# Two of six second layers in three reduced-precision products, and a new order around them, in the last stage of a fused graph and expert network

## The chip, the cores and the metric

The kernel runs on one core of a Trainium2 chip. The metric is the device time of one execution in microseconds, here the median of several runs. The inputs are 8192 tokens of 128 channels (128 graphs of 64 nodes) and an adjacency matrix per graph.

## The reference

Two rounds, each a graph layer and an expert layer, each on a layer norm of the stream `x` and added to it. The last expert layer is the one that matters here:

```
xn = layernorm(x)
rh = relu(xn @ router_w1 + router_b1)
p  = softmax(rh @ router_w2 + router_b2)          # 6 experts
top_w, top_i = top_k(p, 2);  g = softmax(top_w)
h1 = relu(xn @ expert_w1[e] + expert_b1[e])       # 128 -> 128, all e
h2 = relu(h1 @ expert_w2[e] + expert_b2[e])       # 128 -> 128
o  = h2 @ expert_w3[e] + expert_b3[e]             # 128 -> 128
x  = x + sum over the two chosen e of g * o[e]
```

The graph layer before it multiplies the normed stream by the weight and the degree-normed adjacency of each graph.

## The kernel before, in words

The program has three parts: the first round's graph layer, attention and router (to about 260 us), the first expert layer in 71 blocks of 256 slots (to about 535 us), and the last stage, which does the second round's graph layer and its dense expert layer over 16 groups of 512 tokens. The change lies in the last stage, and a little in the preparation of its weights on GpSimd during the blocks.

In the last stage every engine runs its own loop `body(g, p)` over steps. A step holds work of several groups: `g[0]` is the newest, `g[1]` the one before it, and so on. Each operation is a small function that first waits on semaphores and then issues its instructions, and the order in `body` is the order in the engine's queue. VectorE's and GpSimd's steps are numbered two ahead: what is `g[2]` there is `g[0]` in TensorE's step at the same time. The names, for one group:

- graph layer: `aT` (TensorE, adjacency), `tT` (ScalarE copies it out of PSUM), `gnn` (TensorE), `x3` (VectorE adds it to the stream), `st1`, `mv1`, `var1` (VectorE, statistics), `rstd1` (GpSimd, writes `rs_d`), `f3` (VectorE, the normed stream), `f3T` (TensorE, transposes), `hi` (ScalarE) and `lo` (VectorE), which split it into a high and a low half in fp32r; `pick`, `add0`, `add1`, `st0`, `mv0`, `var0` (VectorE), `rstd0` (`rs_c`), `xb` and eight gathers `gt` (GpSimd), `scale` and `xn` (VectorE) prepare the next group's graph layer.
- router: `rh` (TensorE), `rhr` (ScalarE), `logits` (TensorE), a chain of small operations on VectorE with `etop` and `ep` on ScalarE between them, down to `gate`, `ghi`, `glo`; then `gateT` (TensorE) and `gTc` (ScalarE).
- experts, n = 0 to 5: `a(n)` is the first layer, always three fp32r products (high by high, high by low, low by high; line 2205), `ra(n)` (ScalarE, line 1455) its bias and relu into `h1[n % 3]`; `b(n)` is the second layer, one fp32 product, which the trace shows as two records (line 2229), `rb(n)` (ScalarE, line 1462) its bias and relu into `h2[n % 3]`; `m(n)` (VectorE, line 1804) multiplies by the broadcast gate; `c(n)` (TensorE, line 2237) is the third layer, fp32, added up over n in one bank; `eb` adds the last biases, `oTc`, `oT`, `ob` bring the result back and add it to the stream.

An operation reuses a buffer or a PSUM bank as soon as its last reader has signalled. `h1` has three buffers, so `ra(n)` waits for `b(n - 3)` of the same group, or `b(n + 3)` of the group before. The first layers of experts 4, 2 and 1 are computed one step ahead (`a(4, g[0])`, `a(2, g[0])`, `a(1, g[0])` at the end of TensorE's step), but `ra(4)` runs only in the next step, behind `hi`.

The order in TensorE's step: aT, a(0), c(1), c(2), gnn, gateT, c(3), b(0), c(4), a(3), c(5), a(5), eb, b(1), oT, f3T, b(2), b(3), rh, b(4), a(4), logits, a(2), b(5), c(0), a(1).

Of the kernel before, what the change touches and what calls it, by code (L numbers as in the profile page):

```python
# [20 lines left out]
P = 128  # L21
NB, NN, C = 128, 64, 128
TOK = NB * NN
TG = 4
# [72 lines left out]
def build(nc, x, adj_t, gnn0_w, gnn0_b, ln1, ln2, wqkv, wo, router0, w13, w2, gnn1_w, gnn1_b,  # L97
# [19 lines left out]
    with ExitStack() as whole:  # L117
# [906 lines left out]
        with ExitStack() as ctx:  # L1024
# [41 lines left out]
            tile_aT, tile_tT, tile_gnn = sem("tile_aT"), sem("tile_tT"), sem("tile_gnn")  # L1066
            AHEAD = LOOPED + 5
            DEG_BLOCK, degrees = 8, sem("degrees")
            PREPARED = 8 + TG - 1
            st_a, mv_a, var_a, rs_a = sb("st_c", [P, TG, 6]), sb("mv_c", [P, TG, 2]), sb("var_c", [P, TG]), sb("rs_c", [P, TG])  # L1070
            st_b, mv_b, var_b, rs_b = sb("st_d", [P, TG, 6]), sb("mv_d", [P, TG, 2]), sb("var_d", [P, TG]), sb("rs_d", [P, TG])
            rhT = sb("rhT", [P, GT])
# [2 lines left out]
            z, zr, pk, dp, ep, e1 = sb("z_c", [P, TG]), sb("zr", [P, TG]), sb("pk", [P, TG, 2]), sb("dp", [P, TG]), sb("ep", [P, TG]), sb("e1", [P, TG])  # L1075
            rk, ohr, gate = sb("rk", [P, TG, 2]), sb("ohr_c", [P, TG, 2, 8]), sb("gate", [P, TG, 32])
            h1 = [w[:, 1, 0:2, :].rearrange("p c r -> p (c r)") for w in (act1, prod)] + [sb("h1_2", [P, GT])[:, :]]
            h2 = [f[:, :, :].rearrange("p t c -> p (t c)") for f in flat] + [act1[:, 0, 0:2, :].rearrange("p c r -> p (c r)")]
            h2g = [xs[:, 0:2, :, :].rearrange("p u t c -> p (u t c)"), ys[:, :, :, :].rearrange("p u t c -> p (u t c)"),
                   prod[:, 0, 0:2, :].rearrange("p c r -> p (c r)")]  # L1080
            oT = sb("oT", [P, GT])
            gateT = [sb(f"gateT{i}", [P, P]) for i in range(2)]
            gateS = [sb(f"gateS{i}", [P, GT], f32r) for i in range(2)]
            spare, spare2 = sb("spare_c", [P, 1]), sb("spare_d", [P, 8])
# [20 lines left out]

            per = {n[0].rstrip("012345"): Steps(sem("per_" + n[0]), " ".join(n)) for n in (
                ("a4", "a2", "a1", "a0", "a3", "a5"),
                ("ra2", "ra0", "ra1", "ra3", "ra4", "ra5"),
                ("b0", "b1", "b2", "b3", "b4", "b5"),
                ("rb0", "rb1", "rb2", "rb4", "rb3", "rb5"),  # L1110
                ("m0", "m1", "m2", "m3", "m4", "m5"),
                ("c0", "c1", "c2", "c3", "c4", "c5"))}

# [2 lines left out]
            def reused(engine, by, n, g):  # L1116

                if n >= 3:
                    engine.wait_ge(per[by].sem, per[by].at(f"{by}{n - 3}", g))
                elif has(g - 1):  # L1120
                    engine.wait_ge(per[by].sem, per[by].at(f"{by}{n + 3}", g - 1))
# [23 lines left out]
            def later(g, n):  # L1145
                return None if isinstance(g, int) and g < n else g
# [32 lines left out]
            with nc.Block() as block:  # L1179
# [103 lines left out]
                def _(pool):  # L1283
# [16 lines left out]
                    def weights():  # L1300
# [21 lines left out]
                        pool.wait_ge(ld_w, 16 * NW)  # L1322
                        for high, w in ((ew1_hi, ew1), (rw1_hi, rw1), (eb3_hi, eb3)):
                            G.tensor_copy(high[:, :], w[:, :]).then_inc(prepared, 1)
                        pool.wait_ge(prepared, 4)
                        for low, w, high in ((ew1_lo, ew1, ew1_hi), (rw1_lo, rw1, rw1_hi), (eb3_s, eb3, eb3_hi)):
                            G.tensor_tensor(low[:, :], w[:, :], high[:, :].bitcast(f32), ALU.subtract).then_inc(prepared, 1)
                        pool.wait_ge(prepared, 7)
                        G.tensor_copy(eb3_s[0:16, :], eb3_hi[0:16, :].bitcast(f32)).then_inc(prepared, 1)
                        pool.wait_ge(prepared, 8)  # L1330
                        for t in range(1, TG):
                            G.tensor_copy(eb3_s[32 * t:32 * t + 32, :], eb3_s[0:32, :].bitcast(f32)).then_inc(prepared, 1)
                        pool.wait_ge(prepared, PREPARED)
# [38 lines left out]
                    def rstd1(g):  # L1372
                        if g is not None:
# [2 lines left out]
                                pool.wait_ge(at["f3"], g)  # L1376
                            G.tensor_tensor(rs_b[:, :], var_b[:, :], mhalf[:, 0:TG], ALU.pow).then_inc(at["rstd1"], 1)  # L1377

                    def body(g, p):
                        gt(7, g[1], p[1])  # L1380
                        if isinstance(g[0], int) and g[0] == 2:
                            for n in range(4):
                                gt(n, 2, p[0])
                            rstd1(0)
                            for n in range(4, 7):
                                gt(n, 2, p[0])
                            rstd0(1)
# [17 lines left out]
                def _(act):  # L1405
# [44 lines left out]
                    def ra(n, g):  # L1450

                        if g is not None:
                            act.wait_ge(per["a"].sem, per["a"].at(f"a{n}", g))
                            reused(act, "b", n, g)
                            S.activation(h1[n % 3][:, :], banks[B_A[n]][:, :], ACT.Relu, bias=eb1[:, n:n + 1]).then_inc(per["ra"].sem, 1)  # L1455

                    def rb(n, g):

# [61 lines left out]
                    def body(g, p):  # L1520
                        tT_(later(g[0], 1))
                        ra(0, g[1])
                        rb(5, g[2])
                        gTc(g[1], p[1])
                        ra(1, g[1])
                        rb(0, g[1])
                        ra(3, g[1])
                        oTc(g[2])
                        rb(1, g[1])
                        hi(later(g[0], 1), p[0])  # L1530
                        ra(4, g[1])
                        ra(5, g[1])
                        rb(2, g[1])
                        rhr(g[0])
                        rb(4, g[1])
                        etop_(g[0])
                        ra(2, g[0])
                        rb(3, g[1])
                        ep_(g[0])

                    blocks(act, block_of, 1)
                    hi(0, 0)
# [5 lines left out]
                def _(dve):  # L1548
# [243 lines left out]
                    def m(n, g, p):  # L1792

                        if g is not None:
# [8 lines left out]
                            reused(dve, "c", n, g)  # L1803
                            V.tensor_tensor(h2g[n % 3][:, :], h2[n % 3][:, :], gate_bc[p][:, n, :], ALU.mult).then_inc(per["m"].sem, 1)  # L1804

                    def lg_(g):
                        if g is not None:
                            dve.wait_ge(at["logits"], g + 1)
# [111 lines left out]

                    def body(g, p):
                        opens = isinstance(g[2], int) and g[2] == 0
                        pick(later(g[0], 3), p[0])
                        var1(later(g[2], 1))
                        add0(later(g[1], 2), p[1])
                        f3_(later(g[2], 1))
                        add1(later(g[1], 2), p[1])
# [28 lines left out]
                        gate_(g[2])  # L1956
                        ghi_(g[2])
                        glo_(g[2])
                        x3(later(g[1], 1), p[1])
                        m(4, g[3], p[3])  # L1960
                        st1(later(g[1], 1))
# [86 lines left out]
                def _(pe):  # L2048
# [159 lines left out]
                    def b(n, g):  # L2208

                        if g is not None:  # L2210
# [13 lines left out]
                            elif n == 5:  # L2224
                                if exists(g - 1):
                                    pe.wait_ge(at["ob"], g)
                                else:
                                    pe.wait_ge(per["ra"].sem, per["ra"].at("ra3", g))
                            T.matmul(banks[B_B[n]][:, :], ew2[:, n * C:(n + 1) * C], h1[n % 3][:, :], start=True, stop=True).then_inc(per["b"].sem, 1)  # L2229

                    def c(n, g):

# [21 lines left out]
                    def body(g, p):  # L2254
# [5 lines left out]
                        gateT_(g[1])  # L2260
                        c(3, g[2])
                        b(0, g[1])
                        c(4, g[2])
                        a(3, g[1], p[1])
                        c(5, g[2])
                        a(5, g[1], p[1])
                        eb(g[2], p[2])
                        b(1, g[1])
                        oT_(g[2])
# [70 lines left out]
```

## Time and profile before

| | |
|---|---|
| median of 3 runs | 855.23 us (853.64 to 855.93) |
| the profiled execution | 854.43 us, span 852.5 us |
| TensorE busy | 811.2 us, 95% of the span |
| its weight loads | 624.2 us, 73%, beside the matmuls |
| VectorE busy | 697.4 us, 82% |
| ScalarE busy | 521.3 us, 61% |
| GpSimd busy | 426.0 us, 50% |
| chain that ended last | TensorE 61%, issue 4%, GpSimd 3%, VectorE 1% |

The span is the time from the first to the last instruction in the trace. The chain is followed back from the last instruction, at each step to what released it. Busy shares are averages over three parts with different limits; of the last stage they tell little, and its own stretches have to be asked for.

### The profile page before, as it was taken

What the parts mean: (1) busy time and instruction counts of PE and PEld (TensorE: products, weight loads), DVE (VectorE), ACT (ScalarE), POOL (GpSimd) and SP (SyncE); (2) the same over time, 40 slices, a digit from 0 to 9 for tenths busy, and PEclk for the clock granted to TensorE, in tenths of its full rate; (3) what the DMA queues carried; (4) which work ended last, traced back from release to release, by engine and by line L of the source; (5) the groups of instructions that cost most, each with busy time, mean ns of one, the idle gap of its engine ahead of it and who ended that gap; (6) DMA issues with size and microseconds to landing.
All of it is one profiled execution on the core that took longest, in us unless ns stands there. A gap on an engine that the chain in (4) does not pass through costs nothing.

```text
span 852.5 us, 21598 instructions
## 1 busy us (share of the span) xinstructions
PE 811.2 (95%) x6244; PEld 624.2 (73%) x6245; DVE 697.4 (82%) x2699; ACT 521.3 (61%) x1120; POOL 426.0 (50%) x413
## 2 busy tenths in 40 slices
PE   7998999999788899999999999899999999999997
PEld 7675777777547899999999999566665655555563
DVE  4899988989867798877777888888888888888863
ACT  3666787786645466556565654556566656655664
POOL 4248888888877300940100042566665566666300
PEclk9899999999999999999999999999999999999999
DMA  9602411131115766676666762344443344443323
GB/s 269 178 12 78 114 52 48 54 112 42 45 42 171 201 189 174 172 194 167 174 170 163 176 181 75 111 123 124 122 124 120 118 138 147 152 131 121 108 88 99
DMA packets 107591, 108.25 MB, mean 127 GB/s; under 512 B 27822, under 2 KB 89600, under 8 KB 105344
## 3 DMA queue, kind: packets, MB, share of 16 engines
q1 hardware_dynamic: 96976, 88.52, 36.4%
q0 software_dynamic: 8880, 18.19, 7.0%
q8 instruction: 36, 0.59, 0.3%
q10 hardware_dynamic: 1664, 0.66, 0.3%
q14 instruction: 35, 0.29, 0.1%
HBM read 82.07 MB, written 25.26 MB: 126 GB/s over the span
## 4 chain that ended last, share of the span: by engine, by line
PE 61%; issue 4%; POOL 3%; DVE 1%; DMA 1%; ACT 0%; SPq 0%; POOLq 0%; DVEq 0%
PE banks L2073 16%; PE banks L2113 10%; PE banks L2237 10%; PE banks L2229 9%; PE banks L2205 7%; PE banks L2088 2%; PE banks L2134 2%; PE banks L2145 1%; PE banks L2162 1%; PE banks L2251 1%; PE banks L2174 1%; POOL slots_in L1292 1%; POOL expert_rows L1352 1%; PE banks L2154 1%; DMA slots_out<-ys 0%
## 5 line engine op out<-in xcount | busy, mean ns | idle before, releaser
L1352 POOL DMA_INDIRECT expert_rows<-slots_out,slot_c x128 | 140.8, 1100 | 74.6 <-DVE ys L1610 42.1
L326 POOL DMA_INDIRECT slots_in<-flat,slot_now x115 | 120.7, 1050 | 35.7 <-issue 31.2
L2073 PE MATMUL banks<-xT_hi,w_hi 128*128 128x256 f32 (+1 forms) x426 | 127.0, 298 | 0.4 <-DVE w_lo L1629 0.4
L2073 PE MATMUL banks<-xT_hi,w_lo 128*128 128x256 f32 (+1 forms) x426 | 120.7, 283 | 0.0
L2073 PE MATMUL banks<-xT_lo,w_hi 128*128 128x256 f32 (+1 forms) x426 | 120.4, 283 | 0.0
L2113 PE MATMUL banks<-w_sb,prod 128*128 (+1 forms) x852 | 107.1, 275 | 2.4 <-DVE ys L1610 2.4
L2113 PEld LDWEIGHTS banks<-w_sb,prod 128*128 128x128 f32 (+1 forms) x852 | 101.3, 191 | 2.8 <-issue 2.6
L2073 PEld LDWEIGHTS banks<-xT_hi,w_hi 128*128 128x128 f32 (+1 forms) x426 | 76.2, 179 | 0.6 <-issue 0.6
L2073 PEld LDWEIGHTS banks<-xT_lo,w_hi 128*128 128x128 f32 (+1 forms) x426 | 76.6, 180 | 0.0
L2073 PEld LDWEIGHTS banks<-xT_hi,w_lo 128*128 128x128 f32 (+1 forms) x426 | 76.2, 179 | 0.0
L1426 ACT ACTIVATE w_hi<-w_raw 128x684 fp32r<-128x684 f32 x71 | 54.9, 773 | 26.3 <-PE banks L2073 26.3
L1436 ACT ACTIVATE xT_hi<-banks,ln 128x256 fp32r<-128x256 f32 x71 | 33.7, 475 | 59.4 <-PE banks L2088 58.7
L2205 PE MATMUL banks<-f_hi,ew_hi 128*128 128x512 f32 x96 | 65.2, 679 | 0.5 <-ACT prod L1455 0.5
L828 PE MATMUL banks<-hT,wq 128*128 128x512 f32 x128 | 60.3, 610 | 3.2 <-DVE sc L594 3.2
L1629 DVE TENSOR_TENSOR w_lo<-w_raw,w_hi 128x684 fp32r<-128x684 f32 x71 | 63.0, 887 | 0.0
L1377 POOL TENSOR_TENSOR rs_d<-var_d,mhalf 128x4 f32<-128x4 f32 x16 | 17.9, 1120 | 86.1 <-DVE var_d L1774 86.1
L1462 ACT ACTIVATE flat<-banks,eb 128x512 f32<-128x512 f32 x64 | 43.7, 685 | 20.3 <-DVE ys L1804 15.1
L1362 POOL TENSOR_TENSOR xb_c<-x,gb 128x512 f32<-128x512 f32 x16 | 20.6, 1285 | 70.5 <-DVE x L1702 70.1
L1442 ACT ACTIVATE act<-banks 128x512 f32<-128x512 f32 x71 | 42.6, 600 | 19.9 <-PE banks L2073 19.9
L1610 DVE COPY ys<-banks 128x256 f32<-128x256 f32 x71 | 30.0, 423 | 27.3 <-PE banks L2113 22.6
L1638 DVE TENSOR_TENSOR prod<-banks,act 128x512 f32<-128x512 f32 x71 | 48.9, 689 | 0.5 <-PE banks L2073 0.5
L1626 DVE SCALAR_TENSOR_TENSOR xT_lo<-banks,ln,xT_hi 128x256 fp32r<-128x256 f32 x71 | 34.2, 481 | 14.1 <-ACT xT_hi L1436 14.0
(306 smaller groups left out, 2116.7 us busy)
## 6 DMA issues: line engine op xcount, KB each, us to landing
w_raw<-in_w SPq DMA_DIRECT2D x71, 342.0 KB, 3.4
f_all<-gates_dram SPq DMA_DIRECT2D x16, 1024.0 KB, 6.7
xs<-slots_in SPq DMA_DIRECT2D x71, 128.0 KB, 2.6
slots_out<-ys SPq DMA_DIRECT2D x71, 128.0 KB
f_all<-gates_dram SPq DMA_DIRECT2D x16, 512.0 KB, 4.5
base_all<-in_x SPq DMA_DIRECT2D x16, 256.0 KB, 4.2
out<-ob SPq DMA_DIRECT2D x16, 256.0 KB
slots_in<-zrow SPq DMA_DIRECT2D x20, 128.0 KB, 3.5
```

Source lines behind the costliest of these rows:

```text
L326: G.indirect_dma_start(out=slots_in, out_offset=bass.IndirectOffsetOnAxis(ap=slot_now0[g % 2][:, n:n + 1], axis=0), in_=flat[g % 2][:, n / ...
L828: T.matmul(banks[bank][:, :], wq[:, n * P:(n + 1) * P], hT[:, :], start=True, stop=True).then_inc(done, 1)
L1352: G.indirect_dma_start(out=rows[p][:, n, :], out_offset=None, in_=slots_out[0:filled(g) * R, :], in_offset=bass.IndirectOffsetOnAxis(ap=sl ...
L1426: S.activation(w_hi[:, u % 2, :], w_raw[:, u, :], ACT.Copy).then_inc(w_hi_done, 1)
L1462: S.activation(h2[n % 3][:, :], banks[B_B[n]][:, :], ACT.Relu, bias=eb2[:, n:n + 1]).then_inc(per["rb"].sem, 1)
L1629: V.tensor_tensor(w_lo[:, u % 2, :], w_raw[:, u, :], w_hi[:, u % 2, :].bitcast(f32), ALU.subtract).then_inc(w_lo_done, 1)
L1638: V.tensor_tensor(prod[:, par, 0:2, :].rearrange("p c r -> p (c r)"), banks[3 + 3 * par][:, :], act1[:, par, 0:2, :].rearrange("p c r -> p ...
L2073: last = T.matmul(banks[bank][0:m, half * R:(half + 1) * R], ww[:, par, n * HIDP + c * P:n * HIDP + c * P + m], xx[:, par, :], start=q == ...
L2113: last = T.matmul(banks[7][:, t * P:(t + 1) * P], prod[0:widths[c], par, c, t * P:(t + 1) * P], w2_sb[0:widths[c], bass.ds(e * (KC * C) + ...
L2205: last = T.matmul(banks[B_A[n]][:, :], ww[:, w], ff[p][:, :], start=q == 0, stop=q == 2)
L2229: T.matmul(banks[B_B[n]][:, :], ew2[:, n * C:(n + 1) * C], h1[n % 3][:, :], start=True, stop=True).then_inc(per["b"].sem, 1)
L2237: T.matmul(banks[B_C][:, :], ew3[:, n * C:(n + 1) * C], h2g[n % 3][:, :], start=n == 0, stop=False).then_inc(per["c"].sem, 1)
```

## The change

1. For experts 2 and 4 (`SPLIT`), the second layer's weights and its input `h1` are split into a high and a low half in fp32r, and `b(n)` becomes three fp32r products. The weights are split once, on GpSimd. ScalarE writes `h1_hi` beside `h1` (one activation more in `ra(2)` and `ra(4)`), and `low(n)` subtracts: `low(2)` on VectorE behind `glo`, `low(4)` on GpSimd at the start of its step, behind the last gather.
2. `h1[4]` gets a buffer of its own, and `ra(4)` moves one step ahead, behind `rb(4)`. `rb(3)` moves behind `ep`.
3. TensorE: `a(3)` stands ahead of `c(4)` and `a(5)` ahead of `c(5)`.
4. VectorE: `var1` stands ahead of `pick`.

```diff
-            PREPARED = 8 + TG - 1
+            SPLIT = (2, 4)
+            PREPARED = 8 + TG - 1 + 2 * len(SPLIT)
...
+            h1 = [h1[0], h1[1], h1[2], h1[0], xs[:, 2:4, :, :].rearrange("p u t c -> p (u t c)"), h1[2]]
...
+            ew2_hi, ew2_lo = sb("ew2_hi", [P, len(SPLIT) * C], f32r), sb("ew2_lo", [P, len(SPLIT) * C], f32r)
+            h1_hi = dict(zip(SPLIT, (w_hi[:, 0, 0:GT], w_hi[:, 1, 0:GT])))
+            h1_lo = dict(zip(SPLIT, (w_lo[:, 1, 0:GT], xT_hi[:, :, :].rearrange("p t r -> p (t r)"))))
...
 # GpSimd, preparation of the weights
+                        for i, n in enumerate(SPLIT):
+                            G.tensor_copy(ew2_hi[:, i * C:(i + 1) * C], ew2[:, n * C:(n + 1) * C]).then_inc(prepared, 1)
...
+                        for i, n in enumerate(SPLIT):
+                            w = ew2[:, n * C:(n + 1) * C]
+                            G.tensor_tensor(ew2_lo[:, i * C:(i + 1) * C], w, ew2_hi[:, i * C:(i + 1) * C].bitcast(f32), ALU.subtract).then_inc(prepared, 1)
...
 # GpSimd, the loop
+                    def low(n, g):
+                        if g is not None:
+                            pool.wait_ge(per["ra"].sem, per["ra"].at(f"ra{n}", g))
+                            G.tensor_tensor(h1_lo[n], h1[n], h1_hi[n].bitcast(f32), ALU.subtract).then_inc(per["l"].sem, 1)
                     def body(g, p):
                         gt(7, g[1], p[1])
+                        low(4, g[3])
...
 # ScalarE
                             act.wait_ge(per["a"].sem, per["a"].at(f"a{n}", g))
-                            reused(act, "b", n, g)
-                            S.activation(h1[n % 3][:, :], banks[B_A[n]][:, :], ACT.Relu, bias=eb1[:, n:n + 1]).then_inc(per["ra"].sem, 1)
+                            if n in (1, 4):
+                                if has(g - 1):
+                                    act.wait_ge(per["b"].sem, per["b"].at(f"b{n}", g - 1))
+                            else:
+                                reused(act, "b", n, g)
+                            if n in SPLIT:
+                                S.activation(h1_hi[n], banks[B_A[n]][:, :], ACT.Relu, bias=eb1[:, n:n + 1])
+                            S.activation(h1[n][:, :], banks[B_A[n]][:, :], ACT.Relu, bias=eb1[:, n:n + 1]).then_inc(per["ra"].sem, 1)
...
                         hi(later(g[0], 1), p[0])
-                        ra(4, g[1])
                         ra(5, g[1])
                         rb(2, g[1])
                         rhr(g[0])
                         rb(4, g[1])
+                        ra(4, g[0])
                         etop_(g[0])
                         ra(2, g[0])
+                        ep_(g[0])
                         rb(3, g[1])
-                        ep_(g[0])
...
 # VectorE (its low(n, g) is GpSimd's with V.tensor_tensor and the semaphore of "k")
+                        var1(later(g[2], 1))
                         pick(later(g[0], 3), p[0])
-                        var1(later(g[2], 1))
...
                         glo_(g[2])
+                        low(2, g[2])
                         x3(later(g[1], 1), p[1])
...
 # TensorE
-                            T.matmul(banks[B_B[n]][:, :], ew2[:, n * C:(n + 1) * C], h1[n % 3][:, :], start=True, stop=True).then_inc(per["b"].sem, 1)
+                            if n in SPLIT:
+                                w_high = ew2_hi[:, SPLIT.index(n) * C:(SPLIT.index(n) + 1) * C]
+                                T.matmul(banks[B_B[n]][:, :], w_high, h1_hi[n], start=True, stop=False)
+                                T.matmul(banks[B_B[n]][:, :], ew2_lo[:, SPLIT.index(n) * C:(SPLIT.index(n) + 1) * C], h1_hi[n], start=False, stop=False)
+                                low, key = (per["l"], f"l{n}") if n in (4,) else (per["k"], f"k{n}")
+                                pe.wait_ge(low.sem, low.at(key, g))
+                                T.matmul(banks[B_B[n]][:, :], w_high, h1_lo[n], start=False, stop=True).then_inc(per["b"].sem, 1)
...
                         b(0, g[1])
+                        a(3, g[1], p[1])
                         c(4, g[2])
-                        a(3, g[1], p[1])
+                        a(5, g[1], p[1])
                         c(5, g[2])
-                        a(5, g[1], p[1])
```

## Rows read from the trace of the kernel before

**Rows 1.** Busy us of each engine in two groups, from c(4) to c(4).
```profile
583.68:602.90 19.22, 19.22 (x81) 11.65 (x80) 16.37 (x84) 11.80 (x24) 12.19 (x12) 1.00 0.44 132
...
641.49:660.92 19.43, 19.43 (x81) 11.59 (x80) 16.55 (x84) 11.68 (x24) 12.44 (x12) 1.00 0.40 130
```
Columns: stretch and its length, then PE, PEld, DVE, ACT, POOL busy with their instructions, granted TensorE clock (1.00 is full), DMA share, GB/s.

**Rows 2.** Weight loads' waits, 560 to 820 us: total us, times, longest.
```profile
PEld banks L2237 <- DVE ys L1804: 11.4, 14, 0.8
PEld banks L2162 <- DVE f_lo L1790: 7.3, 13, 0.6
```

**Rows 3.** TensorE's timeline, a long group: start, us, engine, line, instruction, count.
```profile
643.14 1.02 PE L2237 MATMUL banks<-prod,ew 128*128 128x512 f32 x2
...
644.93 1.02 PE L2229 MATMUL banks<-prod,ew 128*128 128x512 f32 x2
...
646.35 0.64 PE L2154 MATMUL banks<-cst,f 128*128 128x128 f32 x4
646.83 1.02 PE L2229 MATMUL banks<-h,ew 128*128 128x512 f32 x2
647.69 1.02 PE L2229 MATMUL banks<-act,ew 128*128 128x512 f32 x2
648.51 0.50 PE L2162 MATMUL banks<-f_hi,rw_hi 128*128 128x512 f32 x1
...
649.33 1.02 PE L2229 MATMUL banks<-prod,ew 128*128 128x512 f32 x2
```

**Rows 4.** TensorE's timeline, a short group: c(3), c(4), f3T, b(4).
```profile
581.80 1.02 PE L2237 MATMUL banks<-xs,ew 128*128 128x512 f32 x2
...
583.67 1.13 PE L2237 MATMUL banks<-ys,ew 128*128 128x512 f32 x2
...
588.46 0.60 PE L2154 MATMUL banks<-cst,f 128*128 128x128 f32 x4
...
591.31 1.02 PE L2229 MATMUL banks<-prod,ew 128*128 128x512 f32 x2
```

**Rows 5.** VectorE's timeline: f3 short, var1, f3 long, x3.
```profile
586.70 1.12 DVE L1782 TENSOR_SCALAR f<-base_all,mv_d,rs_d 128x128 f32<-128x128 f32 x4 [0.15 <-POOL rs_d L1377]
...
643.25 0.17 DVE L1774 TENSOR_SCALAR var_d<-mv_d 128x4 f32<-128x4 f32 x1
...
644.93 1.34 DVE L1782 TENSOR_SCALAR f<-base_all,mv_d,rs_d 128x128 f32 x4 [0.27 <-POOL rs_d L1377]
...
659.13 1.13 DVE L1750 SCALAR_TENSOR_TENSOR base_all<-banks,deg,xb_c 128x128 f32 x4 [1.55 <-PE banks L2145]
```
In brackets: the engine's idle time before the row, and what ended it.

**Rows 6.** ScalarE's timeline, long group: etop, ra(2), rb(3).
```profile
653.36 0.23 ACT L1491 ACTIVATE etop_c<-dtop_c 128x32 f32<-128x32 f32 x1 [1.30 <-DVE dtop_c L1847]
653.52 0.69 ACT L1455 ACTIVATE h<-banks,eb 128x512 f32<-128x512 f32 x1
654.10 0.68 ACT L1462 ACTIVATE flat<-banks,eb 128x512 f32<-128x512 f32 x1
```

**Rows 7.** GpSimd's timeline, long group: rstd1, xb, the last gather.
```profile
643.58 1.20 POOL L1377 TENSOR_TENSOR rs_d<-var_d,mhalf 128x4 f32<-128x4 f32 x1 [5.00 <-DVE var_d L1774]
...
648.02 1.29 POOL L1362 TENSOR_TENSOR xb_c<-x,gb 128x512 f32<-128x512 f32 x1
...
657.11 1.01 POOL L1352 DMA_INDIRECT expert_rows<-slots_out,slot_c  x1 [0.30 <-issue]
```

**Rows 8.** GpSimd's and VectorE's timelines at 354 us, and w_lo's min/median/max in ns.
```profile
354.60 1.85 POOL L1327 TENSOR_TENSOR ew_lo<-f_all,ew_hi 128x768 fp32r<-128x768 f32 x1
356.40 1.09 POOL L1327 TENSOR_TENSOR rw_lo<-rw,rw_hi 128x128 fp32r<-128x128 f32 x1
...
355.02 2.16 DVE L1629 TENSOR_TENSOR w_lo<-w_raw,w_hi 128x684 fp32r<-128x684 f32 x1
357.10 0.41 DVE L1635 TENSOR_TENSOR prod<-banks,act 86x256 f32<-86x256 f32 x1
...
L1629 DVE TENSOR_TENSOR w_lo<-w_raw,w_hi x71: 852/860/2156, 262.5 to 527.4; 128x684 fp32r<-128x684 f32 x71
```

More of the change, by code:

```diff
@@ L1107, in build @@
                 ("a4", "a2", "a1", "a0", "a3", "a5"),
-                ("ra2", "ra0", "ra1", "ra3", "ra4", "ra5"),
+                ("ra4", "ra2", "ra0", "ra1", "ra3", "ra5"),
                 ("b0", "b1", "b2", "b3", "b4", "b5"),
                 ("rb0", "rb1", "rb2", "rb4", "rb3", "rb5"),
+                ("l4",),
+                ("k2",),
                 ("m0", "m1", "m2", "m3", "m4", "m5"),
@@ L1324, in weights @@
                             G.tensor_copy(high[:, :], w[:, :]).then_inc(prepared, 1)
-                        pool.wait_ge(prepared, 4)
+                        for i, n in enumerate(SPLIT):
+                            G.tensor_copy(ew2_hi[:, i * C:(i + 1) * C], ew2[:, n * C:(n + 1) * C]).then_inc(prepared, 1)
+                        pool.wait_ge(prepared, 4 + len(SPLIT))
+                        for i, n in enumerate(SPLIT):
+                            w = ew2[:, n * C:(n + 1) * C]
+                            G.tensor_tensor(ew2_lo[:, i * C:(i + 1) * C], w, ew2_hi[:, i * C:(i + 1) * C].bitcast(f32), ALU.subtract).then_inc(prepared, 1)
                         for low, w, high in ((ew1_lo, ew1, ew1_hi), (rw1_lo, rw1, rw1_hi), (eb3_s, eb3, eb3_hi)):
                             G.tensor_tensor(low[:, :], w[:, :], high[:, :].bitcast(f32), ALU.subtract).then_inc(prepared, 1)
-                        pool.wait_ge(prepared, 7)
+                        pool.wait_ge(prepared, 7 + 2 * len(SPLIT))
                         G.tensor_copy(eb3_s[0:16, :], eb3_hi[0:16, :].bitcast(f32)).then_inc(prepared, 1)
-                        pool.wait_ge(prepared, 8)
+                        pool.wait_ge(prepared, 8 + 2 * len(SPLIT))
                         for t in range(1, TG):
@@ L1804, in m, with low @@
                             V.tensor_tensor(h2g[n % 3][:, :], h2[n % 3][:, :], gate_bc[p][:, n, :], ALU.mult).then_inc(per["m"].sem, 1)
+                    def low(n, g):
+                        if g is not None:
+                            dve.wait_ge(per["ra"].sem, per["ra"].at(f"ra{n}", g))
+                            V.tensor_tensor(h1_lo[n], h1[n], h1_hi[n].bitcast(f32), ALU.subtract).then_inc(per["k"].sem, 1)
                     def lg_(g):
@@ L2228, in b @@
                                     pe.wait_ge(per["ra"].sem, per["ra"].at("ra3", g))
-                            T.matmul(banks[B_B[n]][:, :], ew2[:, n * C:(n + 1) * C], h1[n % 3][:, :], start=True, stop=True).then_inc(per["b"].sem, 1)
+                            w = ew2[:, n * C:(n + 1) * C]
+                            if n in SPLIT:
[5 more added lines that the diff above has]
+                                T.matmul(banks[B_B[n]][:, :], w_high, h1_lo[n], start=False, stop=True).then_inc(per["b"].sem, 1)
+                            else:
+                                T.matmul(banks[B_B[n]][:, :], w, h1[n][:, :], start=True, stop=True).then_inc(per["b"].sem, 1)
                     def c(n, g):
```

## Prediction, made before the changed kernel was run

> **What bounds the kernel now.** I read the page's shares first (TensorE is the busiest engine), then the busy time in stretches of one group of the last stage, then what the weight loads waited for, then the timelines of TensorE, VectorE, ScalarE and GpSimd over one such stretch. The reader is to see four things.
>
> First, a group takes 19.22 or 19.43 us and TensorE is busy through all of it, at the full granted clock; VectorE works 16.4 to 16.55 us of it, ScalarE about 11.7 and GpSimd about 12.3 [rows 1]. So the last stage lasts about 16 periods of 19.3 us and TensorE sets them. Second, TensorE is not quite free of waits: c(4) waits for m(4), and rh for lo, in every group [rows 2]. Third, in a short group f3T starts long after f3 is ready (f: 586.70 + 1.12 = 587.82, f3T at 588.46), in a long one as soon as it is ready (644.93 + 1.34 = 646.27, f3T at 646.35) [rows 3 to 5]. The groups alternate between the two kinds, about half each. Fourth, behind f3T the path is a chain in both: f3T, hi, lo, rh.
>
> **Price of a product.** A full fp32 layer of 512 columns costs TensorE 0.86 us (b(2) at 646.83, b(3) at 647.69). From c(5) at 643.14 to b(1) at 644.93 stand one such layer and four fp32r products, 1.79 - 0.86 = 0.93, so 0.233 each [rows 3]. Three of them are 0.70. Each split expert therefore takes 0.16 us off TensorE's work, two of them 0.32 per group, if the third product finds its low half ready.
>
> **The change, by stretch of a group.**
>
> *c(3) to f3T.* This is 588.46 - 581.80 = 6.66 us in the short group and 0.08 more in the long one: from c(4), where the stretches of rows 1 begin, f3T is at 588.46 - 583.67 = 4.79 and at 646.35 - 641.49 = 4.86 or 4.87 [rows 1, 3, 4]. The work in it is five fp32 layers (4.30), seven fp32r products (1.63) and the four transposes of oT (0.48), 6.41 in all. The rest, 0.25, is c(4): c(3) and b(0) would end at 581.80 + 1.72 = 583.52, c(4) starts at 583.67 and its first pass streams about 0.10 late behind its weight load. With a(3) ahead of c(4), m(4) has 0.70 us more, and this wait goes; c(5) keeps a(5) ahead of it as well. Short groups: -0.25. In long groups f3 is late next: its chain runs gnn, x3, st1, mv1, var1, rs_d, f3. There only the swap of var1 and pick helps: the two small copies of pick stood just ahead of var_d, worth about 0.11 (bounds 0 and 0.22). Long groups: -0.11.
>
> *f3T to b(4).* It is 2.85 in a short group (591.31 - 588.46) and 2.98 in a long one (649.33 - 646.35) [rows 3, 4]. b(2) gets 0.16 shorter, but rh then waits for lo: in the long group rh's products start at f3T + 2.16 at the earliest, and already do. I give the short group 0.03 and the long group nothing. So b(2)'s saving is nearly all lost to the chain f3T, hi, lo.
>
> *b(4) to the next c(3).* b(4) is 0.16 shorter and nothing else moves; a(4), logits, a(2), b(5) and so on follow each other on TensorE. -0.16 in both. aT's wait for xn has about 0.3 to spare.
>
> Sum: short -0.44, long -0.27, mean 0.355. Fourteen groups in the steady state give 4.97. The last round has no f3T, so both splits count, 0.32. Against it: the first round hangs on the f3 chain and has VectorE's new subtraction in it, +0.17; the preparation of the weights, two casts and two subtractions more on GpSimd around 360 us, I take at +0.2. **Saved: 4.97 + 0.32 - 0.37 = 4.9 us.**
>
> **What is added, and its cover.** ScalarE gets two activations per group. The one for expert 4 moves with ra(4) to behind rb(4): two activations, 1.16 at a spacing of 0.58 (653.52 to 654.10), go into an idle of 1.30 ahead of etop. The one for expert 2 takes the place that rb(3) had ahead of ep, and rb(3) moves behind ep, ending near 655.9 [rows 6]. Behind rb(3) stand tT on ScalarE and m(3) on VectorE; tT ends 0.6 later, near 656.5, and gnn, which needs it, ends only just ahead of x3 at 659.13 and takes 0.9, so it begins near 658 [rows 5]. So no cost; if that cover were gone, ep and all the gates behind it would be 0.58 late, still within the 1.3 or so by which glo (657.58, where VectorE's idle ahead of x3 begins) is ahead of gateT. Taking ra(4) out of the queue behind hi only makes ra(5) and rb(2) earlier.
>
> VectorE's low(2) costs about 0.69, 0.61 to the next start. Behind it in VectorE's queue stand x3, m(4) and all of st1 to f3. It fits in the 1.55 us that VectorE idles ahead of x3 [rows 5], which becomes about 0.8. Cost nothing; without cover it would be 0.61 per group on the f3 chain. GpSimd's low(4) has its nearest row in the xb addition, of the same shape, 1.29 us; behind it in the queue stand rs_d and the gathers. It goes after the last gather (657.11 + 1.01) into an idle of 5.0 us ahead of rs_d [rows 5, 7]: ends near 659.5, rs_d is due at about 662.7. Bounds for its duration: 1.1 (the 128 x 128 subtraction) to 1.85 (the 128 x 768 one) [rows 8], hidden by either. TensorE's new waits, for k2 and l4, come 6 us and more after these are done.
>
> **Where the two subtractions meet.** When GpSimd subtracted ew1's low part at 354.60 for 1.85 us, VectorE's w_lo, with both inputs in SBUF, took 2.16 us in place of 0.86; the product from a PSUM bank at 357.10, beside GpSimd's next subtraction, took its usual 0.41 [rows 8]. So an operation of VectorE with two SBUF inputs stands still while GpSimd reads SBUF. By this row low(2) (two SBUF inputs) could be stopped by low(4), up to 1.3 us, and x3 (a PSUM input) could not. Low(2) starts at 657.58 and low(4) at 658.2 or later, a margin of 0.6: low(2) comes first.
>
> The Trainium skill, "SBUF — State Buffer", section on who interferes with whom, has this as a rule against putting such a pair side by side: a VectorE instruction with two SBUF inputs and a GpSimd one that reads SBUF exclude each other, and whichever issued second blocks until the first is done. By that rule, the trace agrees (2.16 beside 0.86). It gives the slower rival below its mechanism; with the order that I expect it costs nothing.
>
> **Time.** The profiled execution took 854.43 with a span of 852.5, 1.9 outside the span. 854.43 - 4.9 = 849.5. The median of the three runs is 855.23, 0.8 above the profiled one; the reported time is compared with that, so I predict 850.3. If all groups were short, 14 x 0.44 - 0.05 = 6.1 is saved, if all long 14 x 0.27 - 0.05 = 3.7: 849.0 to 851.6 is the forecast's own range.
>
> **Rivals.**
> - *All of it counts* (chance 0.09). If the f3 and lo chains have slack, each group loses 0.32 of products and 0.25 of c(4)'s wait: 0.57 x 14 + 0.32 = 8.3, so 846.9. For it: TensorE is busy throughout. Against: rh waits for lo in every group [rows 2], and f3T for f in the long ones.
> - *The chain takes nearly all* (0.16). If every group becomes a long one and low(2) or low(4) leans on it (x3 one or two tenths late), only b(4)'s 0.16 stays, less what the first round and the preparation cost: 0.16 x 15 - 0.4 = 2.0, so 853.2. For it: VectorE gets 17.1 us of work in a period of 18.9, and the long groups are already bound there. Against: 1.55 idle ahead of x3.
> - *Slower: the subtractions collide* (0.10). If gates come 0.6 us late, or the last gather ends early, low(4) starts first; low(2) then waits for it to end near 659.5, x3 starts near 660.2 in place of 659.13, and f3T is 1.1 late. Less the 0.36, that is 0.7 x 15 = 11, so 866; where it happens in a third of the groups, 858.5. The point from which it decides is low(4)'s start against the end of VectorE's glo. For it: only 0.6 between them, and ScalarE's doubled activations lie ahead of the gates. Against: etop and ep each keep their start.
> - *The split does not run at 0.233* (0.05). The third product sits behind a wait; if its weights are loaded only after it, 0.1 to 0.2 is lost in each and nothing stays but the order of a(3): 853.5. Against: the weight loads of waits long satisfied run ahead elsewhere.
>
> The forecast has 0.60. What the measurement of this kernel tells from no change is about 0.3%, 2.6 us: faster means below 852.7. Faster: the forecast, the first rival and a part of the second and fourth, 0.60 + 0.09 + 0.05 = 0.74. Same: the rest of those and mild collisions, 0.17. Slower 0.09. Range 846.9 to 853.9: it holds the forecast, the first rival and the chain rival, and leaves out the collision.
>
> **What would show it.** Right: periods of 18.8 to 19.15 with TensorE busy throughout; b(2) and b(4) as three products of 0.23 to 0.24 between starts; no wait of c(4) for m(4); a longer wait of rh for lo (0.6 at the longest now); f3T waiting for f in most groups; low(2) at its 0.69 ahead of x3, and low(4) behind it; ScalarE's etop still released by dtop. Wrong: x3 released by low(2) rather than gnn, rs_d released by low(4), TensorE waiting at the third product, or periods that do not move.

## The result and the profile after

| | before | after |
|---|---|---|
| median of five runs | 855.23 us (853.64 to 858.0) | 871.4 us (870.75 to 873.33) |
| the profiled execution | 854.43 us, span 852.5 | 873.3 us, span 871.5 |
| last stage, first f3T to last oT | 314.18 us | 329.50 us |
| 14 steady periods in it | 271.48 | 283.28 |
| first period / tail behind the last f3T | 15.84 / 26.86 | 18.86 / 27.36 |

The changed kernel takes 1.0184 times as long (95% interval 1.0154 to 1.0213), where 850.3 us was forecast. The last stage grew by 15.3 us: 11.8 in the steady periods, 3.0 in the first, 0.5 behind the last. (Its start moves between 532 and 541 us from run to run, whatever the kernel, so the experiments below compare the stage itself.)

The page of after: its span, engines and chain. Before, TensorE held 61% of the chain.

```profile
span 871.5 us, 21739 instructions
PE 813.3 (93%) x6276; PEld 628.6 (72%) x6277; DVE 728.6 (84%) x2715; ACT 536.4 (62%) x1152; POOL 454.6 (52%) x433
PE 38%; issue 12%; POOL 12%; DVE 6%; DMA 1%; ACT 1%; POOLq 0%; DVEq 0%; SPq 0%; ACTq 0%
```

One group of after from f3T to f3T, columns as in [rows 1]. In those, TensorE's busy time equalled the stretch, and VectorE had 16.4 to 16.55. Here TensorE misses 0.9 us and VectorE has 18.9.

```profile
676.94:697.50 20.56, 19.68 (x81) 11.89 (x82) 18.89 (x86) 12.82 (x26) 13.95 (x14) 1.00 0.36 125
```

VectorE's timeline of after around low(2), in a group of 20.7 us and in one of 19.3:

```profile
647.52 0.19 DVE L1941 TENSOR_TENSOR gate<-gate 128x32 fp32r<-128x32 f32 x1
647.63 2.49 DVE L1835 TENSOR_TENSOR w_lo<-h,w_hi 128x512 fp32r<-128x512 f32 x1
650.05 1.11 DVE L1775 SCALAR_TENSOR_TENSOR base_all<-banks,deg,xb_c 128x128 f32 x4
...
568.21 0.68 DVE L1835 TENSOR_TENSOR w_lo<-h,w_hi 128x512 fp32r<-128x512 f32 x1
569.66 1.13 DVE L1775 SCALAR_TENSOR_TENSOR base_all<-banks,deg,xb_c 128x128 f32<-128x128 f32 x4 [0.77 <-PE banks L2177]
```

GpSimd's, for the first of these groups (last gather, low(4), and rstd1 with its wait):

```profile
647.25 1.01 POOL L1364 DMA_INDIRECT expert_rows<-slots_out,slot_c  x1 [0.30 <-issue]
648.29 1.28 POOL L1395 TENSOR_TENSOR xT_hi<-xs,w_hi 128x512 fp32r<-128x512 f32 x1
653.90 1.04 POOL L1389 TENSOR_TENSOR rs_d<-var_d,mhalf 128x4 f32<-128x4 f32 x1 [4.33 <-DVE var_d L1799]
```

Low(2) starts at 647.63, its usual 0.68 would end it at 648.31, and GpSimd's low(4) starts at 648.29. Low(2) then stands until low(4) has ended (649.57) and runs 0.55 more, to 650.12. X3, which had a wait of 1.55 for gnn ahead of it [rows 5], has none: it stands behind low(2). In the second group low(4) started 0.81 after low(2) and both took their own time. 11 of the 16 groups are of the first kind, with low(4) starting 0.63 to 0.66 after low(2), and two of the second (0.81 and 0.82); in the other three low(4) runs 4.5 us or more ahead of low(2). (The expectations of e1 and e2 below count 12 and 3; the rows have 11 and 2.) What TensorE sees of it is f3T waiting for f3, the last link of the chain from x3. Its timeline in after, from f3T to rh's first product:

```profile
656.60 0.65 PE L2186 MATMUL banks<-cst,f 128*128 128x128 f32 x4 [0.46 <-DVE f L1807]
657.01 0.48 PE L2264 MATMUL banks<-w_hi,ew_hi 128*128 128x512 f32 x1
657.33 0.40 PE L2265 MATMUL banks<-w_hi,ew_lo 128*128 128x512 f32 x1
657.56 0.40 PE L2268 MATMUL banks<-w_lo,ew_hi 128*128 128x512 f32 x1
657.80 1.02 PE L2270 MATMUL banks<-act,ew 128*128 128x512 f32 x2
658.77 0.50 PE L2194 MATMUL banks<-f_hi,rw_hi 128*128 128x512 f32 x1
```

The same rows show the split working: b(2)'s third product starts 0.23 after the second, b(3) 0.24 after that, with no wait at either.

### The profile page after: what moved, and what is told of

Its sections match the earlier page's. It is cut to its first block, busy times and chain, and to the rows that moved or that the text cites. A ratio compares the mean times of both kernels' runs of the same rounds, so it can differ in the third digit from the quotient of the medians.

```text
span 871.5 us, 21739 instructions
## 1 busy us (share of the span) xinstructions
PE 813.3 (93%) x6276; PEld 628.6 (72%) x6277; DVE 728.6 (84%) x2715; ACT 536.4 (62%) x1152; POOL 454.6 (52%) x433
## 4 chain that ended last, share of the span: by engine, by line
PE 38%; issue 12%; POOL 12%; DVE 6%; DMA 1%; ACT 1%; POOLq 0%; DVEq 0%; SPq 0%; ACTq 0%
PE banks L2105 16%; PE banks L2145 10%; POOL expert_rows L1364 6%; PE banks L2278 3%; PE banks L2237 2%; PE banks L2120 2%; POOL xb_c L1374 2%; POOL rs_c L1382 1%; PE banks L2270 1%; PE banks L2166 1%; POOL slots_in L1299 1%; DVE base_all L1775 1%; DVE xn_c L1766 1%; PE banks L2177 1%; POOL xT_hi L1395 1%
## 5 line engine op out<-in xcount | busy, mean ns | idle before, releaser
L2237 PE MATMUL banks<-f_hi,ew_hi 128*128 128x512 f32 x96 | 59.3, 618 | 1.0 <-ACT h L1480 0.7
L1461 ACT ACTIVATE act<-banks 128x512 f32<-128x512 f32 x71 | 42.6, 599 | 19.3 <-PE banks L2105 19.3
```

The source lines that it names most:

```text
L1461: S.activation(act1[:, par, 0:2, :].rearrange("p c r -> p (c r)"), banks[1 + 3 * par][:, :], ACT.Silu).then_inc(silu_done, 1)
L2237: last = T.matmul(banks[B_A[n]][:, :], ww[:, w], ff[p][:, :], start=q == 0, stop=q == 2)
```

## The experiments

Periods are those of f3T in the profiled run; "stage" is from the first f3T to the last oT; ratios are to the kernel before on the same chip, with 95% intervals. Every kernel here computes the whole reference.

### Is it the meeting of the two subtractions?

**e1_low4_after_low2**: low(4) may not start before low(2) has ended.

```
  pool.wait_ge(per["ra"].sem, per["ra"].at(f"ra{n}", g))
+ pool.wait_ge(per["k"].sem, per["k"].at("k2", g))
  G.tensor_tensor(h1_lo[n], h1[n], h1_hi[n].bitcast(f32), ALU.subtract)
```

> GpSimd's low(4) also waits for low(2)'s signal, nothing else changes. Theory A (the two subtractions collide: low(2), with two SBUF inputs, stands still while GpSimd's low(4) reads SBUF, 1.8 us in 12 of 16 groups, and x3 and the f3 chain with it): low(2) takes 0.68 us in every group, periods of 18.8 to 19.2 us, 849 to 852 us. Rival B (VectorE's and GpSimd's added work has made their own loop the bound, whoever comes first): still 866 to 872. Rival C (low(4) delays rs_d and the gathers on GpSimd's queue): 871 or more, since low(4) comes later here.

Measured: 855.72 us, ratio 1.0016 (0.999 to 1.0041); stage 314.5; first period 16.15, low(2) 0.68 or 0.69 in all groups. The 14 steady periods last 271.89 in place of 283.28: 11.4 us less, 1.04 for each of the 11 collisions. This is the whole loss against before, and none of the gain. Eight of the 14 periods are 19.42 to 19.53, where 18.8 to 19.15 were forecast.

**e2_low4_later**: one 128 x 1 addition on GpSimd ahead of low(4), no wait.

```
+ G.tensor_tensor(spare3[:, :], mhalf[:, 0:1], mhalf[:, 0:1], ALU.add)
  G.tensor_tensor(h1_lo[n], h1[n], h1_hi[n].bitcast(f32), ALU.subtract)
```

> One tiny GpSimd operation (a 128x1 addition, some 0.2 us) ahead of low(4), no new wait. In the changed kernel low(2) was not stopped where it began 0.81 us ahead of low(4) (3 groups) and was stopped where it began 0.63 to 0.66 ahead (12 groups). Theory A with a deciding distance between 0.66 and 0.81: the distance becomes 0.85 or so, low(2) takes 0.68 everywhere, 849 to 853 us. If low(2) is instead slowed by the gather ahead of low(4), or by something of its own: it stays at 2.49 and the time at 870 to 873.

Measured: 858.68 us, 1.0035 (1.0016 to 1.0053). In the 13 groups in which the two are near each other the distance between their starts became 0.80 or more, low(2) took 0.68 to 0.72 in every group, and the steady periods are those of e1. So 0.15 us of delay does what the wait does. (In 11 of the 13 the small addition itself starts some 0.65 after low(2), where low(4) had stood, and low(2) takes 0.70 to 0.72.) The first period stayed long, 17.85: there low(4) has no low(2) near it, but xn's operations.

**e3_split4**: expert 4 split alone.

```
- SPLIT = (2, 4)
+ SPLIT = (4,)
  ...
- low(2, g[2])
```

> Only expert 4's second layer is in three products; expert 2's is one fp32 product as before, and low(2) and its activation are gone. Order of the work as in the change. Theory A: no partner for low(4), so no stop: by my terms 14 groups x (0.41 short, 0.27 long) = 4.8 us less than before, about 850.5. Theory C (low(4) itself is what delays): 865 or more. If b(2)'s saving is indeed lost to the lo chain, this run equals the one with low(4) behind low(2).

Measured: 859.6 us, 1.0052 (1.0035 to 1.007); eight of the 14 steady periods 19.42 to 19.49, first period 19.16. Without a second subtraction on VectorE nothing is left of the collision in the steady part, and the periods still don't shorten. For the first round, VectorE's timeline of after, beside GpSimd's of the same time:

```profile
544.46 2.93 DVE L1766 TENSOR_SCALAR xn_c<-x,mv_c,xscale 128x128 f32<-128x128 f32 x4
...
545.51 1.28 POOL L1395 TENSOR_TENSOR xT_hi<-xs,w_hi 128x512 fp32r<-128x512 f32 x1
```

The four operations of xn take 1.11 to 1.25 in other groups. They have one tensor in SBUF as input and two scalars per partition, and stood beside low(4) too. The second of the four by itself, and the gather that GpSimd runs ahead of low(4); then xn in e1's first round, beside the same gather, where low(4) waits for low(2):

```profile
544.72 2.16 DVE L1766 TENSOR_SCALAR xn_c<-x,mv_c,xscale 128x128 f32<-128x128 f32 x1
544.40 1.08 POOL L1364 DMA_INDIRECT expert_rows<-slots_out,slot_c  x1 [0.17 <-issue]
...
547.92 1.11 DVE L1767 TENSOR_SCALAR xn_c<-x,mv_c,xscale 128x128 f32<-128x128 f32 x4
547.86 1.08 POOL L1364 DMA_INDIRECT expert_rows<-slots_out,slot_c  x1 [0.18 <-issue]
```

The second operation usually takes 0.34 and would have ended at 545.06. Low(4)'s record starts at 545.51, and the operation stands until low(4) has ended at 546.79. E1 shows that the gather alone does not stop it. So the operation was held for at least 0.45 us before low(4), the next in GpSimd's queue behind the gather, has a record at all.

The stop of xn costs 17.85 - 16.15 = 1.7 us of the first period (e2 against e1). That of after is another 1.0 longer. First periods of after, then of e2, which does the same work but for the small addition, with the columns of [rows 1]:

```profile
537.85:556.70 18.85, 13.76 (x66) 9.95 (x66) 16.66 (x80) 10.41 (x20) 8.80 (x9) 0.91 0.14 45
...
536.81:554.66 17.85, 12.42 (x66) 8.57 (x66) 16.47 (x80) 10.42 (x20) 8.96 (x10) 1.00 0.20 52
```

In after TensorE's clock was granted at 0.50 (1.2 in place of 2.4 GHz) for 3.4 us from 548.61 on, shortly behind an idle of 3.57 us ahead of aT, and the same products kept it busy 1.34 us longer. E2 idled 3.44 us there and kept the full clock. The first period of e3, 19.16, has such a stretch too.

### Why is nothing gained without the collision?

**e5_order_only**: no split, the rest of the change as it is.

```
- SPLIT = (2, 4)
+ SPLIT = ()
  ...
- low(2, g[2])
  ...
- low(4, g[3])
```

> No second layer split, no subtractions and no added activations; the order of a(3), a(5), ra(4), rb(3), var1 and the buffer for h1[4] as in the change. My term for c(4)'s wait and var1: 14 x (0.25 short, 0.11 long) = 2.5 us less, 852.7. If the new order itself were harmful (rb(3) late for m(3), pick late for the gathers): over 856, and theory A would not be the whole.

Measured: 856.68 us, 1.0022 (1.0001 to 1.0043); eight of the 14 steady periods 19.43 to 19.54. The order alone makes the periods as long as the split kernel's of e1: something else than TensorE's work sets them. GpSimd's and VectorE's timelines of e1, then of before, at rstd0 (rs_c):

```profile
696.34 1.03 POOL L1364 DMA_INDIRECT expert_rows<-slots_out,slot_c  x1 [0.16 <-issue]
697.39 1.56 POOL L1382 TENSOR_TENSOR rs_c<-var_c,mhalf 128x4 f32<-128x4 f32 x1
...
697.37 0.68 DVE L1830 TENSOR_TENSOR ys<-flat,f_all 128x512 f32<-128x512 f32 x1
699.09 0.17 DVE L1758 COPY deg<-deg_all 128x4 f32 x1 [1.04 <-POOL rs_c L1382]
```

```profile
649.47 1.02 POOL L1352 DMA_INDIRECT expert_rows<-slots_out,slot_c  x1 [0.16 <-issue]
650.50 1.08 POOL L1370 TENSOR_TENSOR rs_c<-var_c,mhalf 128x4 f32<-128x4 f32 x1
...
650.60 0.68 DVE L1804 TENSOR_TENSOR ys<-flat,f_all 128x512 f32<-128x512 f32 x1
651.71 0.17 DVE L1732 COPY deg<-deg_all 128x4 f32 x1 [0.43 <-POOL rs_c L1370]
```

In both, rstd0 waits behind a gather for its turn on GpSimd. Before, it begins 0.10 ahead of m(1) and takes 1.08; in e1 it begins 0.02 behind m(1) and takes 1.56. VectorE's copy of deg behind it waits 1.04 in place of 0.43, the scaled copy xn is late by this, and TensorE's aT waits for xn. TensorE's timeline of e1 there:

```profile
701.08 0.40 PE L2238 MATMUL banks<-f_hi,ew_lo 128*128 128x512 f32 x1
701.70 1.16 PE L2167 MATMUL banks<-adjt_c,xn_c 128*128 128x128 f32 x8 [0.22 <-DVE xn_c L1767]
```

That is a loop in which TensorE's products have little part: rstd1, gathers, xb, rstd0, xn, aT, gnn, x3, rstd1. It closes in some 19.45 us.

**e6_rs_c_early**: e1, with rstd0 moved ahead of the gather gt(2) on GpSimd, which it stood behind.

```
- gt(2, g[0], p[0])
  rstd0(g[1])
+ gt(2, g[0], p[0])
```

> The change with low(4) behind low(2)'s signal, and on GpSimd rstd0 (rs_c) ahead of the third gather. Theory D (without the collision the kernel is bound by the loop rs_d, gathers, xb, rs_c, scale, xn, aT, gnn, x3, rs_d, in which rs_c takes 1.46 us in place of 1.09 because m(1), with two SBUF inputs, begins just ahead of it): rs_c comes some 0.9 earlier and out of m(1)'s way, aT no longer waits for xn, periods fall from 19.45 to 18.9 to 19.1, the last stage from 314.5 to 307 to 309 us, the time to 848 to 850. Rival (VectorE's order, or the f3 and lo chain alone, sets 19.45): no change, 855.

Measured: 853.31 us, 0.9976 (0.9957 to 0.9995); stage 312.8. In the middle of the stage the periods alternate between 18.99 and 19.47 to 19.58. The loop is open in every second group; in the long ones the early gathers bring low(4) forward onto m(4). GpSimd's and VectorE's timelines of e6:

```profile
679.45 1.27 POOL L1396 TENSOR_TENSOR xT_hi<-xs,w_hi 128x512 fp32r<-128x512 f32 x1
...
680.07 1.20 DVE L1830 TENSOR_TENSOR ys<-flat,f_all 128x512 f32<-128x512 f32 x1
```

M(4) has two inputs in SBUF, ends 0.55 after low(4) does (681.27 against 680.72), as low(2) did, and f3 stands behind it.

**e7_before_rs_c_early**: the same move in the kernel before. **e8_order_rs_c_early**: in the kernel of e5.

> The kernel before with only rstd0 ahead of the third gather. Before, aT waited for xn once in 14 groups: by theory D the loop through rs_c is just not the bound there, so 854 to 855, no change that can be measured. If it gains over 2 us, that loop bound the kernel before as well, and TensorE did not.

> Only the new order (nothing split), and rstd0 ahead of the third gather. Theory D: the order's own worth, c(4)'s wait in every group and var1's 0.1, then shows: periods 19.1 to 19.2, 852 to 853. Against the run with both splits it gives what the products bring.

Measured: e7 854.03 us, 0.9979 (0.9958 to 1.0), periods 19.23 to 19.43. Before has 19.21 to 19.51 and one of 20.23, in which aT waits 0.54 for xn. This one is 19.41 here, and the 14 are 0.96 us shorter in all. E8 851.69 us, 0.995 (0.9928 to 0.9971), periods 18.98 to 19.17, 14 of them 267.63 against e7's 270.52: the new order is worth 0.21 a group once rstd0 no longer waits behind that gather. While it does (e5 against before), the order costs a little (271.82 against 271.48 for the 14).

**e9_split4_rs_c_early**: e3 with rstd0 early, low(4) also waiting for glo.

```
  pool.wait_ge(per["ra"].sem, per["ra"].at(f"ra{n}", g))
+ pool.wait_ge(router.sem, router.at("glo", g))
```

> Only expert 4 split, low(4) behind glo (which also keeps it clear of xn in the first round), rstd0 ahead of the third gather. By my terms it is 0.16 a group under the order alone, 2.2 us, and equal to the run with both splits if b(2)'s saving is lost to the chain f3T, hi, lo: 850 to 851.

Measured: 853.11 us, 0.9967 (0.9946 to 0.9989); in the middle of the stage the periods alternate between 18.99 and 19.49, as in e6. No low(2) is in it, so m(4) beside low(4) alone makes the long ones.

### Keeping the subtractions apart from everything

**e10_low4_before_gt7**: e6 with low(4) one gather earlier, ahead of gt(7). **e11_both_vector**: both low halves on VectorE, low(4) right behind low(2), rstd0 early. **e12_split2_rs_c_early**: expert 2 split alone, rstd0 early.

```
  # e10, GpSimd's body
+ low(4, g[3])
  gt(7, g[1], p[1])
- low(4, g[3])
  # e11, VectorE's body (GpSimd's low(4) taken out)
  low(2, g[2])
+ low(4, g[2])
  x3(later(g[1], 1), p[1])
  # e12 (low(4) taken out)
- SPLIT = (2, 4)
+ SPLIT = (2,)
```

> As the run with rs_c early and low(4) behind low(2), but low(4) ahead of the last gather instead of behind it. There low(4) began at 679.45 and m(4), two SBUF inputs, took 1.20 us at 680.07 in place of 0.68, in the long groups (19.55, against 19.0 in the others). Theory A again: low(4) now runs between low(2) and m(4), beside x3, whose input is in PSUM and which it does not stop; m(4) takes 0.68, all periods 18.9 to 19.0, the last stage near 306 us, the time 848 to 850. If x3 is stopped, or the long groups have another cause: no change, 853.

> Both subtractions on VectorE behind glo, none on GpSimd, rs_c early. Theory A: nothing to collide with; VectorE's idle ahead of x3 (0.85 to 1.9 in the last runs) takes the second 0.61 as well: periods 18.95 to 19.2, 849 to 851.5. If VectorE's work is the bound by then, x3 begins late by up to 0.4 and it is 852 to 855.

> Only expert 2 split (low(2) on VectorE, no GpSimd subtraction), rs_c early. Measures whether b(2)'s 0.16 is lost to the chain f3T, hi, lo: if it is, this equals the order alone (851.7, periods 19.16); if not, 2.5 us less, 849 and 19.0.

| | median us | ratio, 95% interval | steady periods | first period | stage |
|---|---|---|---|---|---|
| e10 | 851.89 | 0.996 (0.9942 to 0.9977) | 18.81 to 19.1 | 18.12 | 309.97 |
| e11 | 850.3 | 0.9939 (0.9916 to 0.9962) | 18.8 to 19.13, one of 20.32 | 16.74 | 309.82 |
| e12 | 851.93 | 0.996 (0.9937 to 0.9983) | 18.97 to 19.17 | 16.15 | 310.28 |

One group each from f3T to f3T, of e8, e10, e11 and e12 in this order, columns as in [rows 1]:

```profile
664.39:683.56 19.17, 19.17 (x82) 11.66 (x80) 16.44 (x84) 11.78 (x24) 12.64 (x12) 1.00 0.44 130
```

```profile
664.96:683.97 19.01, 19.01 (x83) 12.00 (x82) 17.05 (x84) 12.81 (x26) 13.98 (x13) 1.00 0.39 132
```

```profile
666.38:685.33 18.95, 18.95 (x83) 11.99 (x82) 17.58 (x86) 12.84 (x26) 12.78 (x12) 1.00 0.42 138
```

```profile
670.91:690.03 19.12, 19.12 (x82) 11.82 (x81) 17.05 (x85) 12.31 (x25) 12.64 (x12) 1.00 0.43 132
```

TensorE is busy through every one of them again, at the full granted clock. E11's VectorE has 1.14 us more than e8's, and its timeline shows where this is hidden: x3 still waits for gnn.

```profile
677.19 0.69 DVE L1834 TENSOR_TENSOR w_lo<-h,w_hi 128x512 fp32r<-128x512 f32 x1
677.79 0.69 DVE L1834 TENSOR_TENSOR xT_hi<-xs,w_hi 128x512 fp32r<-128x512 f32 x1
678.83 1.13 DVE L1774 SCALAR_TENSOR_TENSOR base_all<-banks,deg,xb_c 128x128 f32 x4 [0.34 <-PE banks L2177]
```

E11 is the version that beats both kernels by the most; its interval overlaps those of e10 and e12, so among the three the runs do not choose. It overlaps that of e8 too (0.9928 to 0.9971; 851.69 us, stage 310.48), in which nothing is split: in the whole time the new order with rstd0 early is seen against before, and what the splits add to it is not. E10 loses 2 us in its first period to its own wait: there low(4), now ahead of gt(7), waits 4.85 us for low(2), the gather behind it is late, and x2's addition and f3 with it. VectorE's timeline of e10:

```profile
549.13 1.14 DVE L1719 SCALAR_TENSOR_TENSOR x2a<-expert_rows,gate_c,base_all 128x128 f32<-128x128 f32 x4 [2.11 <-DMA expert_rows<-slots_out,slot_c]
```

E11 has no such wait. Its second period is 20.32 because TensorE's clock was granted at 0.50 for 3.4 us of it, from 552.06 on; the period and that stretch:

```profile
551.46:571.78 20.32, 20.32 (x82) 13.06 (x83) 17.32 (x86) 12.61 (x25) 13.04 (x13) 0.92 0.40 116
552.06:555.47 3.41, 3.41 (x8) 1.98 (x7) 3.00 (x14) 1.86 (x3) 3.09 (x3) 0.50 0.97 331
```

TensorE had idled 1.95 us just before; e10 idled 3.32 us at the same place and kept the full clock. What decides it is not shown.

**e13_pick_first**: e10 with pick ahead of var1 again, as before the change.

```
+ pick(later(g[0], 3), p[0])
  var1(later(g[2], 1))
- pick(later(g[0], 3), p[0])
```

> As the run with low(4) ahead of the last gather, with pick ahead of var1 again. My term for var1 was 0.11 in each group whose f3T waits for f3: if all groups are such, 1.5 us more than that run; if none is, the same time.

Measured: 852.24 us, 0.9965 (0.9945 to 0.9985); periods 18.77 to 19.0, 14 of them 264.70 against e10's 265.38. The swap is worth nothing.

## Why the prediction was wrong, by its steps

**Where it failed: "a margin of 0.6: low(2) comes first".** The margin was right (0.63 to 0.66 measured, 0.81 and 0.82 in the two groups of the other kind) and the conclusion was not. The step took it that the operation which starts first runs through. But low(2) was stopped for 1.8 us in the 11 groups with a margin of 0.63 to 0.66, which cost 1.04 us each. The row that the step went by could not bear it: there w_lo started after GpSimd's subtraction. Low(2)'s own length, 0.69, stood in the prediction beside the margin of 0.6 and would have warned that the two overlap. That this length is the deciding point is not shown: xn's second operation would have ended 0.45 us ahead of low(4)'s start and stood all the same, and a product that started 0.21 ahead of low(4) ran through (last section). The rival "the subtractions collide" had the place and the size of one collision right (f3T 1.1 late; 1.04 measured; x3 some 0.7 after low(4)'s end; 0.48 measured) and the wrong deciding point: it asked that low(4) start first. It had been given 0.10. Its 866 is short of the 871.4 measured because it still counts the gain, and the first round at no more than 0.17.

The rule of the Trainium skill that the prediction leaned on, "SBUF — State Buffer", who interferes with whom, has the one issued second block. The pair is the right one. The prediction read the order of issue off the starts of the records; low(2)'s starts 0.65 us first, and low(2) stood. This does not decide against the rule, since no row shows when an operation was issued, and xn's rows show a hold that begins before low(4)'s record. It does show that the order of starts can't stand in for the order of issue.

**"aT's wait for xn has about 0.3 to spare".** With the new order m(1) starts just ahead of rstd0 in place of just behind it, and rstd0 takes 1.56 for 1.08. Worked out: with 0.3 to spare the loop over xn stood at 19.35 - 0.3 = 19.05; rstd0's 0.48 makes it 19.5, and 19.45 is measured (e1, e5). The spare time was compared with nothing: the forecast's own 0.355 would already have used it up. This took the whole steady gain, and the move of e6 gives it back, not by making rstd0 shorter (it still takes 1.46 at the median in e11, 1.10 before) but by starting it as soon as its variance is there. The contention is the same from the other side, VectorE first and GpSimd standing.

**"Low(4) hidden by either".** In the first round it lies on xn's four operations, 2.93 for 1.11, and the first period is 3.0 longer: 1.7 for this stop (e2 against e1), 1.0 with the stretch at half clock (after against e2), and 0.31 that the collision-free first round of e1 has as well. The +0.17 given to the first round was for the last of these alone.

**What held.** The forecast of 18.8 to 19.15 for the periods, with TensorE the bound, is what e10 shows, and e11 outside the period at a reduced clock; that they need rstd0 moved was no part of it. Against e7, which differs only in the change itself and the place of low(4), e10's 14 steady periods are 270.52 - 265.38 = 5.14 us shorter, where 4.97 was forecast. Against before, whose 14 hold the period of 20.23, it is 6.1. The stretches come from one profiled execution of each kernel, and a difference of 0.05 a group, as between e13 and e10, should not be read. (The forecast's own range comes to 849.1 to 851.5, worked out again, in place of 849.0 to 851.6.) By term:
- the order of a(3) and a(5): (270.52 - 267.63) / 14 = 0.21 a group (e8 against e7); the forecast had 0.25 in short groups and 0.11 in long ones. The periods of 19.29 and 19.41 in e7 became 19.17 and 19.16 in e8, 0.12 and 0.25 less, which is the other way round: that the mean agrees is in part luck.
- b(2)'s split: nearly lost to the chain f3T, hi, lo, as forecast. E12's 14 periods last 267.34, 0.02 a group less than e8's.
- b(4)'s split: (267.34 - 265.38) / 14 = 0.14 (e12 to e10); forecast 0.16.
- var1 ahead of pick: 0.11 was given for long groups, 0 was measured (e13). With rstd0 early, f3's chain is not last, so the case for which it was priced is gone.
- the last round: e10's tail is 26.47, 0.39 less than before; forecast 0.32.
- low(2) 0.69 and low(4) 1.28 (0.69 and 1.29 forecast), the products 0.23; ScalarE's two activations cost nothing that is seen.
- the preparation: GpSimd has 2 us more work there, and the start of the stage scatters by more than that, so +0.2 is open.

## What to carry to other kernels

Where a VectorE operation with its inputs in SBUF and a GpSimd one that reads SBUF come near each other, do not trust a margin of some tenths of a us between their starts, whichever is first, and look at every round, the first and last ones too: low(2) was stopped at a margin of 0.65, and one of xn's operations by a low(4) whose record starts 0.79 after its own. A semaphore wait of the one for the other (e1) removes the stop. Such a pair is removed altogether by giving both operations to one engine when it has the time (e11: 1.14 us more on VectorE cost nothing here) or by a place on GpSimd that no VectorE operation of this kind can reach. And a bound that reads "TensorE is busy throughout" can have a second loop just below it: e1 and e5 show the same 19.45 with and without the work that was taken off TensorE.

## What was not expected of the hardware

- An operation that had started first was stopped by one that started 0.63 to 0.66 us later, and needed 0.55 us more after the other's end, nearly its whole 0.68. So it had done almost nothing by the time that its record would have ended. M(4) in e6, which started after low(4), needed the same 0.55 behind its end. Xn's second operation was held for at least 0.45 us before low(4)'s record began; there, as with low(2), low(4) stood right behind a gather on GpSimd. That GpSimd holds the memory before its record begins would explain both; that VectorE begins again would not explain xn. Neither was tested by a run of its own.
- The order of starts does not decide by itself: rstd0, started 0.02 behind m(1), stood (1.56 for 1.08) and m(1) ran its 0.68; low(4), started 0.02 ahead of low(2)'s usual end, ran its 1.28 and low(2) stood. In the last round of after, where GpSimd had idled 7.43 us ahead of low(4), a product m that started 0.21 before it ran its 0.68, and low(4) took 1.59 for 1.28:

```profile
845.53 0.68 DVE L1829 TENSOR_TENSOR prod<-act,f_all 128x512 f32<-128x512 f32 x1
...
845.74 1.59 POOL L1395 TENSOR_TENSOR xT_hi<-xs,w_hi 128x512 fp32r<-128x512 f32 x1 [7.43 <-ACT xs L1480]
```

- It is not only operations with two inputs in SBUF: xn's, with one and two scalars per partition, were stopped too, by some 1.8 us. X3, which reads a PSUM bank and xb, ran its usual 1.12 beside low(4) in e10's first round:

```profile
544.22 1.12 DVE L1776 SCALAR_TENSOR_TENSOR base_all<-banks,deg,xb_c 128x128 f32<-128x128 f32 x4
...
544.45 1.28 POOL L1396 TENSOR_TENSOR xT_hi<-xs,w_hi 128x512 fp32r<-128x512 f32 x1 [4.85 <-DVE w_lo L1836]
```
